# The score pass of a graph network's attention layer: gathers over the 784 dense chunks in place of 832 padded ones

## The reference

```python
q = (x @ Wq.T + bq).reshape(n, 8, 16)
k = (x @ Wk.T + bk).reshape(n, 8, 16)
v = (x @ Wv.T + bv).reshape(n, 8, 16)
scores = jnp.einsum('ehd,ehd->eh', q[src], k[dest]) / np.sqrt(16)
seg_max = jax.ops.segment_max(scores, src, num_segments=n)
ex = jnp.exp(scores - seg_max[src])
seg_sum = jax.ops.segment_sum(ex, src, num_segments=n)
weights = ex / seg_sum[src]
weighted_values = v[src] * weights[..., None]
agg = jax.ops.segment_sum(weighted_values, dest, num_segments=n)
out = agg.reshape(n, 128) @ Wo.T + bo
```

## Time and profile before

| | |
|---|---|
| median of 3 runs | 9848.69 us (9845.74 to 9861.95) |
| profiled execution | 9844.29 us, span 9842.6 us |
| mean granted clock of TensorE | 0.733 of full speed |
| PE, weight loads | 66%, 58% of the span |
| DVE | 66% |
| ACT | 20% |
| POOL | 70% |
| HBM, read and written | 62 GB/s over the span |
| layer 3's score pass, first to last product L1660 | 7659.3 to 8696.1 us |

### The profile page before, as it was taken

How to read it: one execution, slowest core, us unless ns; L and a number is a source line. 1 busy time by engine, 2 the same in 40 slices (tenths; PEclk the granted TensorE clock), 3 DMA queues, 4 the chain that set the end, 5 groups by cost and what they waited for, 6 DMA issues and landing times. The chain is left out here.

```text
span 9842.6 us, 166334 instructions
## 1 busy us (share of the span) xinstructions
PE 6515.9 (66%) x37701; PEld 5669.2 (58%) x37702; DVE 6537.4 (66%) x22039; ACT 1958.5 (20%) x5860; POOL 6905.2 (70%) x7269
## 2 busy tenths in 40 slices
PE   6777655556676677539305677767776788876676
PEld 4666644445666566534104666556665688866665
DVE  8555476668777777736205888877777555567777
ACT  0222200001111111112101222322222222222223
POOL 1777777767777777777776777457774677757775
PEclk9999965556655656669656888889998555567777
DMA  0000022222222222234204333222222322234443
GB/s 24 2 2 2 12 52 53 53 62 53 53 53 52 63 53 53 53 76 150 83 2 95 104 103 104 73 54 55 55 55 55 72 53 54 54 80 108 108 108 98
DMA packets 428766, 612.61 MB, mean 62 GB/s; under 512 B 171075, under 2 KB 306455, under 8 KB 427879
## 3 DMA queue, kind: packets, MB, share of 16 engines
q0 software_dynamic: 258560, 490.08, 19.8%
q1 hardware_dynamic: 169539, 114.55, 4.2%
q10 hardware_dynamic: 292, 3.41, 0.1%
HBM read 518.43 MB, written 89.13 MB: 62 GB/s over the span
## 5 line engine op out<-in xcount | busy, mean ns | idle before, releaser
L1094 PE MATMUL hop_sums<-hop_rows,hop_weighted 128*128 x4992 | 1155.8, 404 | 1033.6 <-SPq L1230 612.8
L1051 POOL DMA_INDIRECT hop_rows<-hops,src_gather x1568 | 1479.8, 944 | 497.8 <-issue 471.3
L1094 PEld LDWEIGHTS hop_sums<-hop_rows,hop_weighted 128*128 128x128 f32 x4992 | 992.8, 296 | 1139.6 <-issue 1139.1
L1389 POOL DMA_INDIRECT l_pass_rows<-left_table,k_dst_other x832 | 796.5, 957 | 437.7 <-issue 242.6
L1389 POOL DMA_INDIRECT l_pass_rows<-key_table,k_src_other x832 | 787.8, 947 | 384.0 <-issue 250.5
L1872 POOL DMA_INDIRECT l_weigh_rows<-row_table,l_weigh_ring x832 | 786.5, 945 | 306.8 <-issue 203.8
L1389 POOL DMA_INDIRECT l_pass_rows<-related,k_dst_typed x832 | 786.4, 945 | 303.8 <-issue 256.3
L692 POOL DMA_INDIRECT src_sorted<-src_scatter_records,src_scatter_places x784 | 750.8, 958 | 263.6 <-issue 180.5
L1249 POOL DMA_INDIRECT dst_sorted<-rec,dst_places x784 | 765.3, 976 | 240.1 <-issue 240.1
L1051 POOL DMA_INDIRECT hop_rows<-in_x,src_gather x784 | 741.9, 946 | 254.3 <-issue 235.3
L1128 DVE TENSOR_SCALAR hop_weighted<-k_numbers,k_src_place,src_weight 128x128 f32<-128x128 f32 x2496 | 850.2, 403 | 13.6 <-issue 8.8
(11 more groups left out here) (465 smaller groups left out, 16930.8 us busy)
## 6 DMA issues: line engine op xcount, KB each, us to landing
related<-l_tables_rows SPq DMA_DIRECT2D x50, 1024.0 KB, 4.5
hop_rows<-hops,src_gather POOLq DMA_INDIRECT x1568
l_pass_rows<-related,k_dst_typed POOLq DMA_INDIRECT x832
l_pass_rows<-left_table,k_dst_other POOLq DMA_INDIRECT x832
l_pass_rows<-key_table,k_src_other POOLq DMA_INDIRECT x832
l_weigh_rows<-row_table,l_weigh_ring POOLq DMA_INDIRECT x832
src_sorted<-src_scatter_records,src_scatter_places POOLq DMA_INDIRECT x784, 2.1
hop_rows<-in_x,src_gather POOLq DMA_INDIRECT x784, 2.5
```

Source lines behind the costliest of these rows:

```text
L1051: nc.gpsimd.indirect_dma_start(rows[:, s * G + g, :], None, table_in, bass.IndirectOffsetOnAxis(ap=o.gather[:, c:c + 1], axis=0),).then_in ...
L1094: last = nc.tensor.matmul(sums[:, b, g, :], weighted[:, s % SLOTS, g, :], rows[:, bass.ds(slots[g], 1), :], start=True, stop=True)
L1389: nc.gpsimd.indirect_dma_start(rows[:, s, g, :], None, table, bass.IndirectOffsetOnAxis(ap=index[:, c:c + 1], axis=0),).then_inc(got[s], 16)
```

## The change

Layer 3's pass gets a ring like that of the hops. POOL gathers the 784 dense chunks into 16 groups of places, and the consumers still walk the 208 padded groups. For each group DVE loads four places and the count `need` into registers. Then it waits until `landed` has reached that count, and multiplies chunk by chunk, four products of 128 columns in place of one of 512. SP raises `landed` by one for each dense group as its four gathers land. Ahead of that it issues the loads of the breaks, as before, and then a load of the keys from `key_table` back into an SBUF tile of their own, which the weighing spreads over the edges: the tile with keys and values side by side is now given up after the projection. The values go out unscaled, as a third store for each piece in the projection.

`value_rows` becomes `log_sums`. It clamps the sums, takes their logarithm on ACT, adds the peak, and stores 8 numbers (32 bytes) for each row. The weighing is untouched: it subtracts what it finds in those columns, now peak plus logarithm of the sum.

`read_breaks` no longer picks `other`; `begins` and its transposes are in bf16. `gather`, `slot` and `need` stay in SBUF over the whole kernel, `before` and `ones` only through the sort, and `by_src.other` and `countb` are gone.

```diff
@@ -903,13 +902,11 @@
...
-        pick_columns(nc, picked, zero, lambda q: by_edge[:, q, :, 1], chosen).then_inc(picked_ok, 1)
         pe.wait_ge(found, 2)
-        pe.wait_ge(taken, 1)
         pick_columns(nc, picked, zero, lambda q: starts[:, q, :], chosen).then_inc(picked_ok, 1)
-        pe.wait_ge(taken, 3)
+        pe.wait_ge(taken, 2)
         for q in range(QT):
-            last = nc.tensor.transpose(turned[:, q // 4, q % 4 * P:(q % 4 + 1) * P], o.begins[:, q * TQ:(q + 1) * TQ], k.ident[:])
+            last = nc.tensor.transpose(turned[:, q // 4, q % 4 * P:(q % 4 + 1) * P], o.begins[:, q * TQ:(q + 1) * TQ], k.identb[:])
         last.then_inc(turned_ok, 1)
     @shared.vector
@@ -922,17 +919,14 @@
...
-        nc.vector.tensor_copy(o.other[:, 0:CH].rearrange("p (h c) -> p h c", h=2), picked[:, :, 0:half]).then_inc(taken, 1)
-        dve.wait_ge(picked_ok, 2)
-        dve.wait_ge(taken, 2)
+        dve.wait_ge(taken, 1)
-        nc.vector.memset(o.other[:, CH:], 0)
@@ -1370,6 +1367,14 @@
                     sp.dma_start(brk[s * heads:(s + 1) * heads, here, :],
                                  brk_h[s * length:s * length + NSLOT].rearrange("(a w l) -> a w l", a=1, l=wch * P)
                                  [:, here, 0:length + 1].to_broadcast([heads, count, length + 1])).then_inc(loaded[n], 16)
+            if preload is not None:
+                tile, home = preload
+                sp.dma_start(tile[:], home).then_inc(preloaded, 16)
+            for n in range(GU if ringed else 0):
+                sp.wait_ge(got[n % RING], (n // RING + 1) * 16 * G)
+                sp.sem_inc(landed, 1)
+            if preload is not None:
+                sp.wait_ge(preloaded, 16)
             if reload is not None:
                 tile, home = reload
                 sp.wait_ge(scored, GROUPS)
@@ -1378,11 +1383,11 @@
         @block.gpsimd
         def _(pool):
-            for n in range(GROUPS):
+            for n in range(GU if ringed else GROUPS):
                 s = n % ring
                 if n >= ring:
-                    pool.wait_ge(weighed if at else scored, n - ring + 1)
+                    pool.wait_ge(weighed if at else scored, n - ring + 1 + (NBLK // G if ringed else 0))
                     pool.sem_inc(running, 1)
                 for g in range(G):
                     c = n * G + g
@@ -1652,11 +1657,23 @@
                 if 0 <= t < GROUPS:
                     b = t % 2
+                    if ringed:
+                        slots_of = load_blocks(nc, dve.engine, o.slot[:, t * G:(t + 1) * G], G, RING * G - 1)
+                        need = dve.value_load(o.need[:, t:t + 1], min_val=1, max_val=GU)
+                        dve.wait_ge(landed, need)
+                    else:
+                        dve.wait_ge(got[t % ring], (t // ring + 1) * 16 * G)
                     dve.wait_ge(spread_ok, t + 1)
-                    dve.wait_ge(got[t % ring], (t // ring + 1) * 16 * G)
                     if t >= 2:
                         dve.wait_ge(scored, t - 1)
-                    if att is None:
+                    if ringed:
+                        by_chunk = rows[:].rearrange("p r g f -> p (r g) f")
+                        for g in range(G):
+                            last = nc.vector.tensor_tensor(pair[:, b, g:g + 1, :, :].rearrange("p g h f -> p g (h f)"),
+                                                           own[:, b, g:g + 1, :], by_chunk[:, bass.ds(slots_of[g], 1), :],
+                                                           ALU.mult)
+                        last.then_inc(paired, 1)
+                    elif att is None:
                         nc.vector.tensor_tensor(pair[:, b, :, :, :].rearrange("p g h f -> p g (h f)"), own[:, b, :, :],
                                                 rows[:, t % ring, :, 0:D], ALU.mult).then_inc(paired, 1)
                     else:
@@ -2888,44 +2905,36 @@
-def value_rows(nc, k, total, values, table, bias, name):
...
+def log_sums(nc, k, total, table, bias, name):
+        sums = sb("sums", [P, NBLK, HEADS3])
+        rows = sb("rows", [P, NBLK, HEADS3])
+        clamped = sem("clamped")
+        logged = sem("logged")
+            nc.vector.tensor_single_scalar(sums[:], total[:, 0:NBLK, 0:HEADS3], TINY, ALU.max).then_inc(clamped, 1)
+            dve.wait_ge(logged, 1)
+            nc.vector.tensor_tensor(rows[:], rows[:], total[:, 0:NBLK, HEADS3:2 * HEADS3], ALU.add).then_inc(made, 1)
+        @block.scalar
+        def _(act):
+            act.wait_ge(clamped, 1)
+            nc.scalar.activation(rows[:], sums[:], ACT.Ln).then_inc(logged, 1)
+
+            sp.wait_ge(made, 1)
+            sp.dma_start(table[0:NP, 2 * D:2 * D + HEADS3].rearrange("(b p) f -> p b f", p=P), rows[:]).then_inc(stored, 16)
+            sp.wait_ge(stored, 16)
@@ -3130,18 +3136,20 @@
             def tmp(name, shape, dt=F32):
                 return layer.enter_context(nc.sbuf_tensor(f"l3_{name}", shape, dt))
-            pairs = tmp("keys_values", [P, NBD, 2 * D])
-            keys, values = pairs[:, :, 0:D], pairs[:, :, D:2 * D]
+            keys = tmp("keys", [P, NBD, D])
             with ExitStack() as softmax:
                 total = softmax.enter_context(nc.sbuf_tensor("l3_softmax_sums", [P, NBLK - 1 + G, 2 * HEADS3], F32))
                 queries = softmax.enter_context(nc.sbuf_tensor("l3_queries", [P, NBD, D], F32))
-                scale_row(nc, k, bias3[:, 2 * D:3 * D], float(D // HEADS3) ** -0.5, "l3_scale")
-                norm_project(nc, k, w3[:, 0:3 * D], bias3, [(0, 2 * D, pairs, 1.0),
-                                                            (2 * D, 3 * D, queries, float(D // HEADS3) ** -0.5)],
-                             [(keys, key_table), (queries, row_table[:, 0:D])], "l3_project")
-                softmax_pass(nc, k, by_src, by_src.other, key_table, D, D // HEADS3, None, queries, None, True, total,
-                             None, None, 8, "l3_pass")
-                value_rows(nc, k, total, values, row_table, bias3[:, 3 * D:4 * D], "l3_rows")
+                with ExitStack() as projected:
+                    pairs = projected.enter_context(nc.sbuf_tensor("l3_keys_values", [P, NBD, 2 * D], F32))
+                    scale_row(nc, k, bias3[:, 2 * D:3 * D], float(D // HEADS3) ** -0.5, "l3_scale")
+                    norm_project(nc, k, w3[:, 0:3 * D], bias3, [(0, 2 * D, pairs, 1.0),
+                                                                (2 * D, 3 * D, queries, float(D // HEADS3) ** -0.5)],
+                                 [(pairs[:, :, 0:D], key_table), (queries, row_table[:, 0:D]),
+                                  (pairs[:, :, D:2 * D], row_table[:, D:2 * D])], "l3_project")
+                softmax_pass(nc, k, by_src, by_src.gather, key_table, D, D // HEADS3, None, queries, None, True, total,
+                             None, None, 8, "l3_pass", (keys, key_table.rearrange("(b p) f -> p b f", p=P)), True)
+                log_sums(nc, k, total, row_table, bias3[:, 3 * D:4 * D], "l3_rows")
             free_semaphores(nc, k)
             total = tmp("total", [P, NBD, D])
             weigh_and_sum(nc, k, by_dst, by_dst.other, row_table[0:NP, :], keys, total, "l3_weigh")
```

48 lines of the change are left out of this document (13 added, 35 removed).

## The result

The changed kernel takes 9775.83 us (median of 4 runs, 9768.67 to 9785.07) against 9847.22 for the kernel before (4 runs), a ratio of 0.9931 (95% interval 0.9919 to 0.9944): faster, by 71 us. The forecast was 9826 us and a range of 9782 to 9864. The profiled execution took 9768.67 us (span 9766.9), so 75.6 us less than the one of before.

The account below looks back on a forecast made before the run. POOL's gathers were taken to pace layer 3's pass, with the DVE-PE lockstep a close second limit that would bind next. Pass -16, its end -2.5 and breaks -4.3 made -23, from 9848.7 to 9826 us; range 9782 to 9864.

Parts of the forecast that it names:

- Gathers: Layer 3's pass: 784 gathers in place of 832 take 60 us off POOL, whose pace becomes 4.71 us per group.
- DVE per group: Layer 3's pass: split product, loads, check and wait add 1.3 us in the long chain, 0.95 in the other, nothing elsewhere.
- the pass's start: Layer 3's pass: DVE's first product comes near 7686, late start about 0; third projection store delays the pass by 2 us.
- the breaks: Reading of breaks: one pick gone and bf16 transposes save 4.3 us, all of which comes through.
- Clock: PE in layer 3's pass: more stretches at the full clock take 1.0 us off each window, giving 39.3 us.
- 4.0 elsewhere: Expected sign in layer 3's pass: L1484 distances about 6.5 and 8.1 us in each window, 4.0 in the other groups.
- rival B: POOL still paces layer 3's pass with 979 us of gathers and the chains hide; -65, 9784 us, chance 0.13.
- A: The forecast: layer 3's pass leaves POOL's pace and is bound by DVE-PE chains; 9826 us, 9805 to 9850, chance 0.55.
- Rival C: Slower: each of three new DVE steps costs 0.6 us in both chains, no clock gain; 9885 us, chance 0.12.
- I take 12 from 8729: -2.5: End of layer 3's pass: the small store of 6272 pieces of 32 bytes takes 12 us, saving 2.5; ends -7 and +8.
- comes ahead of its wait and costs nothing: End of layer 3's pass: the logarithm's table load on ACT costs 0, as ACT stands idle through the drain.
- Rival D: Late start isn't eaten up: SP's preload blocks behind the breaks, first count near 7705; +20, 9846 us, chance 0.20.

Follow-up runs that it names:

- e6_const_paced: Changed kernel without register loads on DVE: one product of 512 columns at a constant place, constant waits at the mean pace of the real counts; 0.9931, 9787.4 us.
- e1_three: Changed kernel gathering only three of four chunks per dense group (588 gathers), the fourth place filled with zeros once; 0.9925, 9785.7 us.
- f_three: e1_three repeated on another run's chip beside the changed kernel: 588 gathers, every fourth chunk zeros; 0.9931, 9777.5 us.
- e7_hoist: Changed kernel with DVE's loads of places and need moved ahead of the scan and carries that wait for PE; 0.9931, 9788.0 us.
- e9_products_only: As e6_const_paced, but four products of 128 columns in place of one of 512; 9773.6 us in one execution.
- e10_loads_only: As e6_const_paced, with loads and register wait written in but places unused; in the trace only the need is loaded; 9772.5 us in one execution.
- f_hoist_three: e8_hoist_three repeated on the same chip as f_three: 588 gathers, loads ahead of DVE's waits; 0.9913, 9756.4 us.
- e8_hoist_three: Changed kernel with the edits of e1_three and e7_hoist joined: 588 gathers, loads moved up on DVE; 0.9911, 9754.5 us.
- e2_three_const: As e1_three, also without loads of places and need: one product of 512 columns, constant place and wait; 0.9879, 9737.6 us.
- f_extra_need: Changed kernel with the need alone loaded a second time on DVE for each group; 1.0009, 9851.2 us.

## Why the prediction was wrong

**The chains were right, the term of the clock was wrong.** "Gathers", "DVE per group", the pass's start and the breaks came out nearly as worked. The chains grew by 0.75 and 1.15 us (6.28 and 7.86 against 5.53 and 6.71) where +0.95 and +1.3 were forecast; against the 5.42 and 6.60 of e6_const_paced, which has none of the new work, it is 0.86 and 1.26. A window at the lower clock is 4.0 + 4.0 + 6.28 + 4.47 + 7.86 + 4.63 + 4.0 + 4.65 = 39.9 us, where 40.3 were forecast. The step that failed is "*Clock*": "Bounds: nothing, and 2 us per window (two such gains); I take 1.0." Measured with nothing pacing it (e1_three, f_three), the changed consumer runs at 37.6 to 38.0 us, so the clock gives 1.9 to 2.3 us, at the forecast's upper bound or above it. Of the 1.6 us between the forecast window (39.3) and the changed kernel's (37.7), 0.4 is the chains and 1.2 the clock; over 26 windows the whole is 42 us, and the pass came out 40 below its forecast. In the changed kernel the gains come in the seventh and eighth group: 4.00 to 2.60 and 4.65 to 2.69, 3.4 us together, in 17 of 24 windows. The basis of the forecast was one pair of groups before in which the clock was 0.90.

None of the signs of being wrong that the prediction named came up: the chains grew by 0.75 and 1.15 us ("under 0.5 or over 2"), the clock of the pass was 0.61 ("above 0.65"), the small store took 6.1 us ("20 us"). The one sign that did fail stood among those for it: "4.0 elsewhere", where 2.60 and 2.69 us came.

**So rival B held in its result.** "POOL still paces" was given 0.13 and 9784 us. It was argued away with "it needs 37.7 us per window, less than the 38.0 without any new work", a sum at the lower clock only. e6_const_paced, e7_hoist, e9_products_only and e10_loads_only settle it: their long chains are 6.60 to 7.35 us and the changed kernel's 7.86, and their windows are 37.9 to 38.1 us and the changed kernel's 37.7 to 38.1. What B didn't say, and f_three does, is that the consumers stand at the same place: taking the gathers' limit away gains 0.1 us (9777.7 to 9777.5), taking the loads off the path 0.6 (9788.6 to 9788.0), both less than the runs scatter, and both together 21 us. The forecast's A and B are two limits within 1% of each other.

**Rival C was the neighbour.** It "decides slower from about 41.2 us per window". One more load of the need with its check takes the window to 41.0 and the kernel to 1.0009 of before. C's price of 0.6 us for each of the new steps wasn't met: by the runs it is 0.2 for the places, and 0.35 and 0.75 for the need with its check, in the two chains. In the records of the long chain the need's load starts 0.39 us behind that of the places, part of which lies beside the two short products; from there to the waits it is 0.64 us, of which 0.35 until the check begins. The forecast had 1.05 us for loads, check and wait in the long chain, and the gap is 0.98. The Trainium skill, "DMA: Bandwidth & Descriptors", Latency and other measured facts, has about 600 ns as the floor of a tensor_load; in this trace the records of the two register loads ahead of the product at 8121.96 are 0.35 and 0.31 us long, so it doesn't hold here.

**The stage behind the pass.** "I take 12 from 8729: -2.5" was a term sized wrongly: the store landed after 6.1 us, half of the 12, and the whole stage from L2922 to the first gather takes 11.4 us against 20.7. The end of -7 was too near as well; the rest of the -9.9 is a drain 0.6 us shorter. The pieces were as many as before, 32 bytes each in place of 544, so their number alone did not set the 13 us of before: there 3.41 MB went out, at 255 to 319 GB/s once the transfers ran, now 0.20 MB at about 54. And the store was not what the stage hung on. 8.1 of the 9.3 us that the stage lost lie ahead of the bias add: the reciprocal (2.60), the copy of the peaks (0.37) and the five products (6.95) on DVE are gone, and the add starts 2.3 us behind the start of the clamp in place of 10.4. The forecast had a wrong step beside it: the table's load "comes ahead of its wait and costs nothing". It came ahead of the wait, but ACT began it only as the stage began (8660.22, 1.28 us), so that the logarithm started 0.70 us behind the clamp's end, and the bias add stands behind both. The Trainium skill, "DMA: Bandwidth & Descriptors", Specifications, says that pieces below 512 bytes become a read-modify-write; if they did here, the store still landed in 6.1 us. Its lower rate is in line with that, but the runs don't show what else slows small pieces. Since the bias add ends 0.6 us after the landing, a faster store would gain nothing.

**Rival D fell.** The first product came 7677.2 - 7645.1 = 32 us behind the first gather, as worked (7686 - 7653 = 33), SP's preload took 1.40 us to issue, and POOL's gathers show no pause. A consumer that is late costs nothing while the ring holds what comes in and the producer is the limit.

**Open.** What makes PE's clock rise in the seventh group. It isn't the length of the chains alone: 3 to 10 raised windows with a long chain of 6.6 to 6.9 us, 8 with 7.35, 9 to 17 with 7.86, 1 to 3 with 8.6. Nor is what the clock gives in all: against the sum of a window at the lower clock it is 1.9 to 2.3 us in f_three and e1_three, 0.8 to 1.2 in f_hoist_three and e8_hoist_three (38.2), 1.9 in e2_three_const (37.8) and 0.3 in f_extra_need (41.3). Nor does the count of raised windows hold all of it: in e2_three_const only 0.6 of the 1.9 us lie in the seventh and eighth group, the rest in the first five, and in f_three 1.3 of 1.9. By the medians PE waits 1.3 to 3.2 us in the fifth group of these kernels and then works without a pause through the eighth. That the clock pays a chain back was the theory of these runs; it holds between e8_hoist_three and e1_three, where two thirds of 1.7 us came back, and fails for longer chains.

## What to carry to other kernels

Before a limit is called second, work out what it does at both levels of PE's clock: here groups that ran at the higher level, behind the long chain above all, moved a limit from 39.9 us per window to about 38, onto the first one. What makes them do so is not shown, so the sum gives a range and not a value. When two limits stand within 1%, taking one away gains nothing and proves nothing; take both away in one kernel before judging either. Loads of registers that a later wait or product needs belong ahead of the engine's own wait for another engine, where they cost nothing in the chains (e7_hoist) and 21 us come free once the gathers don't pace either (f_hoist_three); left behind it, the kernel stands one such load from losing its whole gain.
